# The third bf16 part of the edge payload made by GpSimd in SBUF instead of by TensorE and ScalarE

## What is computed

```python
def graph_part(x, src, edge_attr):             # x is layer-normed
    node_feat = relu(x @ W_down.T + b_down)
    time_feat = relu(edge_attr @ W_time.T + b_time)          # 212500 x 64
    sums = segment_sum(time_feat, src, num_segments=n)       # by source node
    counts = segment_sum(ones, src, num_segments=n)
    combined = concat([node_feat, sums / maximum(counts, 1)])
    return x + relu(combined @ W_fusion.T + b_fusion) @ W_up.T + b_up

x = x + graph_part(layernorm(x), ...)
x = x + experts_part(layernorm(x))             # shared MLP + top 2 of 4 experts
```

## Time and profile before

| what | value |
|---|---|
| median of 3 runs | 2281.26 us (2279.72 to 2284.28) |
| the profiled execution: its span | 2527.2 us |
| TensorE busy | 2229.3 us, 88% |
| VectorE busy | 1868.7 us, 74% |
| ScalarE busy | 1324.9 us, 52% |
| GpSimd busy | 1168.9 us, 46% |

### The profile page before, as it was taken

The page is one execution under the profiler, slowest core; times in us unless marked ns, Lnnn a source line. Parts: engine busy times, 40 slices in busy tenths (PEclk is TensorE's granted clock), DMA queues, the critical chain, the costliest instruction groups (busy, mean ns, idle before and its releaser), DMA issues.

```text
span 2527.2 us, 79027 instructions
## 1 busy us (share of the span) xinstructions
PE 2229.3 (88%) x29648; PEld 1866.3 (74%) x29648; DVE 1868.7 (74%) x5668; ACT 1324.9 (52%) x2835; POOL 1168.9 (46%) x940
## 2 busy tenths in 40 slices
PE   5777787899899989999889999997887999999999
PEld 2666665688788778888778888887886777777776
DVE  9875886778888778788766677666997666666665
ACT  2666777656666666666566666652001444444443
POOL 0656686566666576566655666563001111111110
PEclk7889998899999999999999999998998999999999
DMA  2333443466667566676656667665773111111111
GB/s 73 98 102 105 155 137 122 152 180 195 208 202 211 160 186 186 186 217 202 202 147 190 182 197 213 214 186 153 210 208 104 42 53 57 43 52 57 44 51 34
DMA packets 251784, 361.20 MB, mean 143 GB/s; under 512 B 35216, under 2 KB 225354, under 8 KB 250222
## 3 DMA queue, kind: packets, MB, share of 16 engines
q1 hardware_dynamic: 207972, 236.08, 33.9%
q0 software_dynamic: 43200, 119.22, 12.9%
q10 hardware_dynamic: 234, 0.85, 0.1%
HBM read 208.01 MB, written 197.15 MB: 160 GB/s over the span
## 4 chain that ended last, share of the span: by engine, by line
PE 71%; DVE 8%; issue 8%; ACT 5%; DMA 3%; another core or an unknown queue 3%; DVEq 1%; POOL 0%; SPq 0%; ACTq 0%; POOLq 0%
PE bank L673 17%; PE moved L644 16%; PE bank L760 8%; PE bank L630 7%; PE moved L773 6%; PE bank L648 4%; DMA arena<-table 2%; PE bank L768 2%; PE bank L657 2%; ACT arena L1420 2%; ACT arena L1426 2%; PE bank L844 2%; PE bank L800 2%; DVE arena L984 1%
## 5 line engine op out<-in xcount | busy, mean ns | idle before, releaser
L1620 POOL DMA_INDIRECT table<-arena x832 | 1037.8, 1247 | 643.0 <-ACT arena L1426 370.8
L1426 ACT ACTIVATE arena<-moved 128x588 bf16<-128x588 f32 x832 | 545.9, 662 | 252.6 <-PE moved L644 177.5
L644 PE MATMUL moved<-arena 128*128 128x196 bf16 x4992 | 618.5, 261 | 24.2 <-ACT arena L1426 16.4
L644 PEld LDWEIGHTS moved<-arena 128*128 128x128 f16 x4992 | 464.9, 101 | 118.9 <-ACT arena L1426 37.1
L1420 ACT ACTIVATE arena<-bank 128x512 f32<-128x512 f32 x624 | 372.6, 597 | 335.7 <-remote 151.8
L1086 DVE TENSOR_TENSOR sums<-sums,bank 128x130 f32 x960 | 272.8, 284 | 292.1 <-PE bank L673 202.8
L1164 DVE TENSOR_TENSOR arena<-arena 128x3072 f16<-128x3072 f16 x208 | 364.2, 1751 | 50.9 <-PE moved L644 42.5
L673 PE MATMUL bank<-arena,w_all 128*128 128x64 bf16 (+1 forms) x8640 | 347.7, 195 | 53.5 <-issue 44.7
L673 PE MATMUL bank<-arena 128*128 128x64 bf16 (+1 forms) x8640 | 345.1, 195 | 53.2 <-issue 32.8
L673 PEld LDWEIGHTS bank<-arena,w_all 128*128 128x128 bf16 x8640 | 313.2, 99 | 72.1 <-issue 64.1
L673 PEld LDWEIGHTS bank<-arena 128*128 128x128 bf16 x8640 | 312.9, 99 | 67.5 <-issue 47.2
(11 more groups left out here) (229 smaller groups left out, 2685.1 us busy)
## 6 DMA issues: line engine op xcount, KB each, us to landing
arena<-table SPq DMA_DIRECT2D x320, 441.0 KB
arena<-in_attr SPq DMA_DIRECT2D x208, 144.0 KB
table<-arena POOLq DMA_INDIRECT x832
x_ln<-arena SPq DMA_DIRECT2D x98, 128.0 KB
arena<-in_x SPq DMA_DIRECT2D x97, 128.0 KB
arena<-x_ln SPq DMA_DIRECT2D x24, 512.0 KB, 4.6
out_rows<-arena SPq DMA_DIRECT2D x24, 512.0 KB, 3.3
fused_node<-arena SPq DMA_DIRECT2D x98, 32.0 KB
```

The source lines that it names most:

```text
L644: mm = e.matmul(moved8[:, 4 * (n % 2) + h, 0:PW], slot_hot[s % NSLOT][:, t, h * P:(h + 1) * P], upper(s, 0, PW)[:, t, :], start=j == 0, st ...
L1426: e.activation(row_buf[n % NROWS], moved8[:, 4 * (n % 2):4 * (n % 2) + 3, 0:PW], ACT.Copy).then_inc(s_rows, 1)
L1620: e.indirect_dma_start(out=tables[k], out_offset=bass.IndirectOffsetOnAxis(ap=dest[s % NDEST][:, a:a + 1], axis=0), in_=row_buf[n % NROWS] ...
```

## The change

GpSimd makes LOW as MID minus the upper half of MID, both in SBUF (`keep_low`). The second `take_off` and the third `relu_z` are gone, with the semaphore between them, and `features` of the next step waits on MID instead of LOW. GpSimd's `keep_low(step)` stands between its first and its second scatter of the step. It waits on `s_mid` of its step.

```diff
@@ tensor_program
             def features(s):
                 e.wait_ge(s_attr[s % NATTR], 16 * (s // NATTR + 1))
                 if s:
-                    e.wait_ge(s_low, s)
+                    e.wait_ge(s_mid, s)
...
                 for k, n, c in chunks[:third]:
                     add_up(k, n, c)
-                if s < NS:
-                    e.wait_ge(s_mid, s + 1)
-                    take_off(s, MID).then_inc(s_less_mid, 1)
                 if moving:
                     move(s - 1, 2)
@@ scalar_program
                 if moving:
                     keep_rows(GS * (s - 1) + 1)
-                if s < NS:
-                    e.wait_ge(s_less_mid, s + 1)
-                    relu_z(s, LOW).then_inc(s_low, 1)
                 if moving:
                     keep_rows(GS * (s - 1) + 2)
@@ gpsimd_program
+            def keep_low(s):
+                e.wait_ge(s_mid, s + 1)
+                e.tensor_tensor(part_of_pay(s, LOW, A), part_of_pay(s, MID, A), upper(s, MID, A), ALU.subtract).then_inc(s_low, 1)
+
+            e.wait_ge(s_one, NPAY)
             for step in range(n_steps):
+                if step == 0:
+                    keep_low(0)
                 if 0 <= step - 1 < NS:
                     s = step - 1
                     k = part_of[s]
                     e.wait_ge(s_dest, s + 1)
                     for a in range(GS):
+                        if a == 1 and step < NS:
+                            keep_low(step)
                         n = GS * s + a
                         e.wait_ge(s_rows, n + 1)
```

More of the change, by code:

```diff
@@ L110, in gnn_ffn @@
         s_sort, s_code_ps, s_codes = sem("s_sort"), sem("s_code_ps"), sem("s_codes")
-        s_z, s_high, s_less_high, s_mid, s_less_mid, s_low, s_lo = (sem(f"s_{n}") for n in ("z", "high", "less_high", "mid", "less_mid", "low", "lo"))
+        s_z, s_high, s_less_high, s_mid, s_low, s_lo = (sem(f"s_{n}") for n in ("z", "high", "less_high", "mid", "low", "lo"))
         s_slot, s_begun, s_dest_ps, s_dest, s_moved, s_rows = (sem(f"s_{n}") for n in ("slot", "begun", "dest_ps", "dest", "moved", "rows"))
```

## The result

The changed kernel takes 2466.38 us (2461.84 to 2471.08, 4 runs) against 2281.39 us before: a ratio of 1.0812, 95% interval 1.0792 to 1.0832. It is 185 us slower. The forecast was 2510, with 2240 to 2640 as its range.

What follows compares the result with a forecast made beforehand. GpSimd, gaps counted, was taken to bound the changed loop: 6.45 + 1.57 = 8.02 us a step, 1669 us against 1444 in the runs, +225 on 2281 giving 2506, forecast as 2510 us; range 2240 to 2640.

Steps and rivals of the forecast that it cites:

- GpSimd as the bound: In the loop, GpSimd's need rises from 6.45 to 8.02 us a step and sets the pace; 2480 to 2640 us, chance 0.60.
- The sign named for it: Profile after: GpSimd waits on ScalarE's copies almost nowhere; TensorE and ScalarE wait on GpSimd's L1608, the subtraction.
- Its price: GpSimd's added subtraction: 1.27 us from an fp32 add plus a 0.30 us gap, 1.57 us a step; ordinary upper end 1.85.
- Its gap is gone: Sign of being wrong: GpSimd's subtraction takes under 1 us or lacks the 0.30 us gap charged to it.
- The 246 us: Profiled span 2527.2 us minus median 2281.3, taken as loop stalls of the profiled execution only; loop in runs 1444 us.
- TensorE's 76 us: Dropping one L648 matmul (50 us) and half its wait on ScalarE (26 us); earned only if TensorE is the bound afterwards.
- I add nothing for it: VectorE's loss beside the subtraction, between nothing and 1.27 us a step, was charged at nothing in the forecast.
- my upper end of 1.27: Most VectorE could pay per step: the whole subtraction of 1.27 us, giving 7.93 us, just under GpSimd's new sum.
- the likeliest case: GpSimd sets the loop's pace after the change: 2480 to 2640 us, chance 0.60.
- partly hidden: Rival: the profile stretches all engines alike, GpSimd needs 7.24 against 6.94 us a step; 2343 us, range 2286 to 2480, chance 0.13.
- Faster: Rival: GpSimd still has room, TensorE stays the loop's bound and its 76 us are earned; 2205 us, chance 0.17.
- The lock: Rival: VectorE's one-hot work and GpSimd's subtraction take turns, 9.42 us a step, 2796 us in all, chance 0.07.

Runs made afterwards that it cites:

- r6: Changed kernel without its subtraction (LOW zeroed once, third part left out), on a chip where the kernel before takes 2282.79 us: 2258.10 us, 0.9899 of before.
- r7: Kernel before plus an idle GpSimd memset of 1.36 us per step, reading no SBUF: 2444.33 us against 2282.79, 1.0714.
- r2: Changed kernel without its subtraction (LOW zeroed once), on a chip where the kernel before takes 2523.88 us: 2509.85 us, 0.9924 of before.
- r1: Kernel before, unchanged, profiled again: 2525.32 us in the profiled execution, median 2523.88 us in 17 runs without a profile.
- r9: Kernel before, unchanged, profiled on another chip: 2554.38 us in the profiled execution, 2562.77 us in 23 runs.
- r3: Kernel before plus an idle GpSimd subtraction per step, its result read by nobody: 2641.26 us against 2523.88, 1.0438.
- r4: Kernel before plus an idle GpSimd memset of 0.82 us per step, reading no SBUF: 2539.90 us against 2523.88, 1.0054.
- r10: Kernel before plus an idle GpSimd subtraction per step, its result read by nobody, on another chip: 2643.97 us against 2562.77, 1.0333.
- r12: Changed kernel with the subtraction on GpSimd in one step of four, the third part made as before in the others: 2582.61 us against 2562.77, 1.0080.

## Why the prediction was right

**GpSimd as the bound.** Right, and shown. The sum said that GpSimd is taken 6.45 us a step, and that TensorE's gain would be covered. r6 shows GpSimd 97% taken with no subtraction at all, and r7 shows that its time alone lengthens the loop, after 0.45 us a step that were free. The sign named for it came too: GpSimd waits on ScalarE's copies 92 us in place of 371, and `move` waits on L1608.

**Its price.** The step "with the gap of 0.30 us ... the price is 1.57 us" was too high. The subtraction took 1.15 us on the mean in place of 1.27, median 1.06, with no gap ahead and 0.17 behind. Against the gap of 0.30 us that stood between the same two scatters before, that is 1.15 + 0.17 - 0.30 = 1.02 us a step, 114 us less than charged. "Its gap is gone" was one of the signs of being wrong, and it came true ahead of the subtraction. Two terms that I had at nothing made up for most of it. GpSimd's other instructions rose by 29 us (the scatters from 1247 to 1291 ns, 37 us, the zero writes fell by 8). And GpSimd is not taken to the full: busy 1352 us and 232 us of gaps leave 48 us of waiting. So 1669 - 114 + 29 + 48 = 1632 us is the loop as measured, and 37 of the 44 us between 2510 and 2466. That the forecast came within 2% is thus in part luck. The rise of the scatters is not the subtraction's doing: without it they take 1293 ns in r6 and 1281 in r2, and beside the memset, with the three rounds kept, 1248 ns in r7. Its cause is open.

**The 246 us.** The step "I take it that the stalls belong to the profiled execution" was wrong. r1 and r9 show the same time with and without a profile. The stalls are in the runs as well, on two of the three chips timed. The subtraction of 246 us gave the right loop for the median all the same, by luck: the median was of a chip without them. r6's loop of 1420 us and its 25 us make 1445, where I had 1444. The forecast that the span would stay near 2506 to 2564 us came from that wrong step and was not tested, because the profile after is of the other kind of chip. The times expected of r2, r3 and r4 rested on it too; those of r10 and r12 were written for the faster kind of chip and fell on the slower.

**TensorE's 76 us.** The removal gives 25 us (r6). I had said that what I gave it is covered, and it is: GpSimd is nearly full already in the kernel without the subtraction. Whether the 76 us were there to be had at all is not shown; r2 gains 14 us where GpSimd waits 331 us on ScalarE's copies.

**VectorE.** "I add nothing for it" is close for the time and wrong for the engine. Its busy time in the loop rose by 202 us, 0.97 us a step, near my upper end of 1.27. The Trainium skill, SBUF — State Buffer, section "Who interferes with whom", says that the two exclude each other when VectorE has two SBUF inputs and GpSimd reads SBUF. The trace agrees: 1.55 us in place of 0.54 beside the subtraction, and a largest L1067 of 592 ns beside the memset. The page also says that whoever issues first gets the port for the whole instruction. In the rows above, the VectorE instruction started at 745.07 and the subtraction at 745.13, and it was VectorE's that took 1.0 us longer, so by the recorded starts the trace differs. It does so in an orderly way. In 148 of the 208 steps the lengthened VectorE instruction had started first, by up to 0.69 us, and the earlier it started, the longer it took (1.0 us more with a lead of 0.06 us, 1.55 more with 0.6). In the 16 steps where an L1161 had a lead of 0.77 us or more, it kept its length and the subtraction was late. So the order that decides looks like that of the records with the subtraction put some 0.7 us earlier; what it does in that time no record shows.

**The rivals.** By the number alone, 2466 us lies just below the 2480 to 2640 us of the likeliest case and inside the 2286 to 2480 us that I had given to "partly hidden"; it takes the experiments to tell them apart. Faster and partly hidden fell with r6 and r7: the 0.30 us between scatters counts in the runs too. The lock works on both sides, as its sign said (L1161 at 1942 ns, L1063 at 645), but with the dependency it is worth 22 to 47 us by r7 against the changed kernel, not 9.42 us a step.

**A reading of the rows.** Against the rival "faster" I wrote that GpSimd was taken for 5.9 us in the step of the earlier trace rows. From 740.96 to 746.55 there are three scatters, and a step has four. With the fourth it is 7.2 us, and with 1.57 us more 8.7 against TensorE's 7.2. The argument was stronger than I made it.

What stays open: how much of the 81 to 117 us of the idle subtraction on the slower chips is the hold on VectorE. A memset of the same length was not run there, only the shorter one that cost 0 to 16 us. In r3 GpSimd is busy 1366 us of a loop of 1807, about as long as in r7, and with its gaps only 88% taken, so there its pace alone doesn't explain the loss. Why those chips are slower is open as well; the traces show only gaps on TensorE at full granted clock and waits whose releaser isn't found.

## What to carry to other kernels

Count the gaps between an engine's instructions as its time: GpSimd read as 64% busy, and was some 93% taken in the runs, by my estimate (1342 of 1445 us). Before moving work to an engine, remove the work from its old place alone: if that gains less than the instructions removed, look in that profile for an engine with no waiting left, since it may be the one that is to take the work. And compare a profile's span with the runs' median before using one for the other: they may be of different chips.

## What I had not expected of the hardware

- Two times for the same program, by the chip: 2281 to 2283 us and 2524 to 2563 us. Where it is slower, 0.82 us of GpSimd work in each step costs 0 to 16 us.
- GpSimd's subtraction with a strided bf16 operand (1063 ns median) is quicker than its one add of fp32 at the same size in the earlier trace rows (1271 ns), and quicker than the same subtraction with a bf16 result in r3 (1297 ns).
- A GpSimd memset never lengthens VectorE's instructions with two SBUF inputs, a GpSimd subtraction does, in 148 of 208 steps by 0.9 us or more: 202 us in all.
- A scatter is held by VectorE, and to the same point each time: in the trace of before, 168 of the 169 scatters that started while L1164 ran, at least 0.3 us before its end, ended 0.83 to 0.87 us after it, whatever their start. L1164 itself was never longer than 1.82 us.
